# The scan's input products in pairs, with eight state buffers in place of six

## The chip, the cores and the metric

The kernel runs on one core of a Trainium2 chip. The metric is the device time of one launch in microseconds (us), the median of several runs. The engines are called by their names in the profile: PE (TensorE matmuls) and PEld (its weight loads), DVE (VectorE), ACT (ScalarE), POOL (GpSimd) and SP (SyncE, which issues all transfers). Each runs its own queue in order; they meet through semaphores.

## The reference

The reference is a network of two layers on x of 32 sequences x 256 tokens x 128 features, all in fp32. Each layer has the form

```python
h = layernorm(x) * (1 + ca) + sa;  x = x + ga * mixer(h)
h = layernorm(x) * (1 + cb) + sb;  x = x + gb * ffn(h)
```

with shifts, scales and gates per sequence. Layer 0: attention with 16 query heads, 4 key heads and a relative position bias, then a mixture of 16 experts with 4 picked per token. Layer 1: a selective scan over 256 channels x 16 states, then three chained matrices and a tanh. The scan is what the change touches:

```python
dA  = exp(dt[..., None] * A)
dBx = dt[..., None] * B_ssm[:, :, None, :] * x_conv[..., None]
# h[t] = dA[t] * h[t-1] + dBx[t]
y = einsum('btdn,btn->btd', h, C_ssm)
```

## The kernel before

The 32 sequences are worked in 16 pairs of 512 tokens (TOK). Every phase of a pair (attention `a_`, experts `m_`, scan `s_`, last block `f_`) is cut into small functions, one for each piece and engine. A written timetable puts each piece at a step: a pair starts every 128 steps (STEPS), and `AT` holds a due step relative to the pair's start for each function. Each engine walks over all steps from -101 to 2455 and emits what is due, in a fixed order within a step (`step_sync`, `step_gpsimd`, ...). A step is thus a place in a queue, not a time. Four pairs are in flight at a time: while pair p is scanned, pair p+1 goes through its experts and the pairs behind through attention. The last three pairs have tables of their own (`LAST_AT`, `LATE_SCAN`, `LATE_LAG`), since nothing new starts behind them.

The scan of a pair has 256 x 16 = 4096 rows of 512 tokens, which makes 32 batches of 128 rows. A row of the partition axis is a channel and a state: 16 channels x 8 states. One fetch (`s_fetch_sync`, L1145) brings dt and dt*x of 16 channels, each repeated on 8 partitions (512 KB), into a ring slot; the ring has four. A fetch serves two batches, one for each half s of the states: of eight batches the first four use fetches n to n+3 with s = 0, the next four the same fetches with s = 1. Batch m is due at step 388 + 27m/8 of its pair (at smaller numbers in the last two pairs). It consists of

- the fetch, due at lag -14 (-12 in the last three pairs). It waits until POOL's product (`s_dbx`) and ACT's decay (`s_da`) of the last batch of the slot's former contents are done.
- the decay on ACT (`s_decay_scalar`, L1186), lag -1: exp of dt times A into a PSUM bank. It waits for the scan of the batch before (of the one before that in the last two pairs, which have two banks).
- the input product on POOL (`s_input_gpsimd`, L1197), lag -3: (dt*x) times B into a state buffer `hb[at % HB]`. It waits for the fetch, for the row of B in `bc`, and for the sum that frees the buffer.
- the scan on DVE (`s_scan_vector`, L1203), lag +1, in place in the state buffer.
- the product with C, in place: on POOL (`s_read_gpsimd`, L1210), lag +4, or in the late pairs on DVE (`s_read_vector`, L1218).
- for every fourth batch, the sum of four batches over the states on PE (`s_sum_tensor`, L1233), lag +6. It frees four state buffers.

Other pieces named later: on POOL the experts' weighing (`m_weigh_gpsimd`, L929) and four root chains per pair (`ln_root_gpsimd`, L436 to L453: 16 dependent operations on 128x4 elements), due at steps 155 (b), -82 (a), 330 (n) and 517 (f) of their pairs; on ACT th (L900) and the attention's exp (L605); on DVE L907 and L922 of the experts, the routing (L759 to L814), L663, and the scan's end L1240 and L1242; on PE L872, L916 and L934 (the experts' matmuls) and L588 (scores). L1313 adds the last block to its input, L1317 stores it.

Of the kernel before, what the change touches and what calls it, by code (L numbers as in the profile page):

```python
# [9 lines left out]
ALU = mybir.AluOpType  # L10
# [3 lines left out]
P = 128  # L14
B, T, D = 32, 256, 128
PAIRS = B // 2
TOK = 2 * T
# [28 lines left out]
BATCHES = 32  # L46
HB = 6
XSLOTS = 3
RING = 4
# [18 lines left out]
def build(nc, dram, out, q_rows, w_rows_d, dt_rows, bc_rows):  # L68
    ctx = ExitStack()
    with ctx:  # L70
# [82 lines left out]
        bc = sb("bc", [P, 2 * SG, TOK])  # L153
        work = sb("work", [P, HB * TOK + RING * 2 * TOK])

        def cut(lo, n):
            return work[:, lo:lo + n]

        hb = [cut(k * TOK, TOK) for k in range(HB)]
        ring = [cut((HB + 2 * k) * TOK, 2 * TOK).rearrange("p (r t) -> p r t", r=2) for k in range(RING)]  # L160

        conv_s, conv_t = step[:, 0, :], step[:, 2, :]
        dt_s = [step[:, 0, :], step[:, 2, :]]
# [78 lines left out]
        s_in = [sem(f"s_in{k}") for k in range(RING)]  # L242
        s_da, s_dbx, s_h, s_hc, s_y, s_g, s_yv = (sem("s_" + n) for n in ("da", "dbx", "h", "hc", "y", "g", "yv"))
# [13 lines left out]
        def tokens(ap):  # L257
# [15 lines left out]
            x_res_sync=107, a_store_sync=-34, m_store_sync=178, m_fetch_sync=-13, s_rows_sync=377,  # L273
            s_rows_in_sync=[378, 380, 384, 386], s_store_sync=[372, 374], s_fetch_sync=-14, f_store_sync=531,
            a_scores_tensor=0, m_gate_tensor=1, m_up_tensor=3, m_down_tensor=9, a_turn_tensor=5, a_values_tensor=40,
# [13 lines left out]
            s_silu_vector=[352, 359], s_zgate_vector=[392, 401], f_res_vector=514, f_stats_vector=518, f_end_vector=533,  # L289
            s_read_gpsimd=4, m_weigh_gpsimd=5, s_input_gpsimd=-3, a_root_gpsimd=-82, b_root_gpsimd=155, s_root_gpsimd=330,  # L290
            f_root_gpsimd=517, s_step_vector=[366, 370],
# [50 lines left out]
        LATE_LAG = dict(s_decay_scalar=0, s_scan_vector=1, s_read_gpsimd=4,  # L342
                        s_input_gpsimd=-3, s_sum_tensor=6, s_fetch_sync=-12)

# [811 lines left out]
        def landed(p, n):  # L1156
            return 16 * (FETCHES // RING * p + n // RING + 1)
# [31 lines left out]
        def s_input_gpsimd(pool, p, m):  # L1189
            n, j, s = batch(m)  # L1190
            at = BATCHES * p + m
            if m in (0, 4):
                pool.wait_ge(bc_in[s], 16 * (p + 1))
            pool.wait_ge(s_in[n % RING], landed(p, n))
            if at >= HB:
                pool.wait_ge(s_y, (at - HB) // 4 + 1)
            nc.gpsimd.tensor_tensor(hb[at % HB], ring[n % RING][:, 1, :], bc[:, s, :], ALU.mult).then_inc(s_dbx, 1)  # L1197

# [425 lines left out]
        def step_gpsimd(pool, st):  # L1624
            at = batch_due("s_read_gpsimd", st)
            if at is not None and not copies(*at):
                s_read_gpsimd(pool, *at)
            at = expert_due("m_weigh_gpsimd", st)
            if at is not None:
                m_weigh_gpsimd(pool, *at)  # L1630
            at = batch_due("s_input_gpsimd", st)
            if at is not None:
                s_input_gpsimd(pool, *at)
            p = due("a_root_gpsimd", st)
            if p:
                ln_root_gpsimd(pool, LN_A, p)
            p = due("b_root_gpsimd", st)
            if p is not None:
                ln_root_gpsimd(pool, LN_B, p)
            p = due("s_root_gpsimd", st)  # L1640
            if p is not None:
                ln_root_gpsimd(pool, LN_S, p)
            p = due("f_root_gpsimd", st)
            if p is not None:
                ln_root_gpsimd(pool, LN_F, p)
# [241 lines left out]
```

## Time and profile before

| | us |
|---|---|
| median of 3 runs | 2771.68 |
| lowest and highest run | 2770.18, 2782.97 |
| span of the profiled execution | 2781.6 |

The profiled execution's own time is not given apart from its span; of the three times the highest lies 1.4 us above the span. The page gives busy times of the engines over the span, the costliest groups of instructions, and the idle time before each with its releaser. Shares over the whole span hide that the kernel has a long steady part (about 240 to 2400 us, one pair each 157 us) and an end of some 280 us in which no new pair comes in.

### The profile page before, as it was taken

How to read it: one execution, taken by the hardware profiler on the slowest of the kernel's cores; microseconds unless marked ns; L12 is line 12 of the kernel's file. 1: busy time of each engine (PE TensorE's matmuls, PEld its weight loads, DVE VectorE, ACT ScalarE, POOL GpSimd, SP SyncE). 2: the span in 40 equal slices, each digit the busy share in tenths (PEclk: the TensorE clock that was granted, in tenths of full speed). 3: DMA queues.
4: the chain of work that ended last, by engine and by line, in shares of the span. 5: the costliest groups of instructions: out<-in, count | busy, mean ns of one | idle time of the engine just before them, and what ended most of it. 6: DMA issues, size and time to landing. Idle time of an engine off the chain costs nothing. (4 is left out here: it accounts for less than half of the span.)

```text
span 2781.6 us, 37104 instructions
## 1 busy us (share of the span) xinstructions
PE 2360.3 (85%) x9792; PEld 1217.4 (44%) x9792; DVE 1947.1 (70%) x3193; ACT 1630.6 (59%) x4157; POOL 1717.8 (62%) x2235
## 2 busy tenths in 40 slices
PE   5889998989888999989899898988989898987533
PEld 3555544444444444444444444444444444432110
DVE  2445558686877868686776768677686867768776
ACT  3655656666666666666666665666666566643432
POOL 1012258585866858585776757587685757766643
PEclk9999999999999999999999999999999999998755
DMA  7424365565546565555556465554645555344542
GB/s 135 48 46 78 58 141 99 122 125 126 118 84 134 115 132 114 111 121 118 115 109 134 95 121 119 119 117 85 143 106 120 115 125 105 85 116 114 126 122 68
DMA packets 497980, 304.96 MB, mean 110 GB/s; under 512 B 349817, under 2 KB 416297, under 8 KB 497321
## 3 DMA queue, kind: packets, MB, share of 16 engines
q1 hardware_dynamic: 497772, 302.59, 53.4%
q8 instruction: 82, 1.34, 0.2%
q14 instruction: 126, 1.03, 0.1%
HBM read 242.21 MB, written 26.74 MB: 97 GB/s over the span
## 5 line engine op out<-in xcount | busy, mean ns | idle before, releaser
L1197 POOL TENSOR_TENSOR work<-work,bc 128x512 f32<-128x512 f32 x512 | 648.1, 1274 | 100.1 <-PE bank L1233 92.1
L1203 DVE TENSOR_TENSOR_SCAN work<-bank,work 128x512 f32<-128x512 f32 x512 | 621.3, 1213 | 96.4 <-POOL work L1197 74.7
L929 POOL TENSOR_TENSOR zh<-zh,w_bc 128x512 f32<-128x512 f32 x256 | 326.7, 1276 | 582.9 <-DVE zh L922 582.8
L1186 ACT ACTIVATE bank<-work,neg_a 128x510 f32<-128x510 f32 x512 | 351.5, 687 | 457.1 <-DVE work L1203 445.5
L1210 POOL TENSOR_TENSOR work<-work,bc 128x512 f32<-128x512 f32 x436 | 564.9, 1301 | 80.6 <-DVE work L1203 80.5
L588 PE MATMUL bank<-ke,q_all 96*128 96x256 f32 x2048 | 558.3, 396 | 12.1 <-DMA q_all<-q_rows 12.1
L605 ACT ACTIVATE probs<-bank,nmax 128x256 f32<-128x256 f32 x1024 | 473.7, 470 | 131.3 <-DVE nmax L595 129.3
L595 DVE TENSOR_REDUCE nmax<-bank 128x2 f32<-128x512 f32 x512 | 348.6, 681 | 229.6 <-PE bank L588 218.5
L588 PEld LDWEIGHTS bank<-ke,q_all 96*128 96x128 f32 x2048 | 384.3, 198 | 215.9 <-issue 164.6
L916 PE MATMUL bank<-h_b,w_t 128*128 128x512 f32 x512 | 296.9, 663 | 119.5 <-DVE zh L907 110.2
L615 PEld LDWEIGHTS bank<-ident,probs 128*128 128x128 f32 x2048 | 256.0, 144 | 241.9 <-issue 173.7
L623 ACT ACTIVATE probs_t<-bank 128x512 f32<-128x512 f32 x512 | 304.0, 594 | 85.9 <-PE bank L645 69.7
L615 PE MATMUL bank<-ident,probs 128*128 128x128 f32 x2048 | 318.9, 279 | 37.5 <-ACT probs_t L623 37.3
L907 DVE SCALAR_TENSOR_TENSOR zh<-th,bank 128x512 f32<-128x512 f32 x256 | 174.5, 682 | 233.2 <-ACT th L900 231.7
L872 PE MATMUL bank<-h_b,w_t 128*128 128x512 f32 x512 | 291.1, 651 | 0.0
L934 PE MATMUL bank<-zh,w_t 128*128 128x512 f32 x512 | 265.3, 600 | 0.9 <-POOL zh L929 0.9
L922 DVE SCALAR_TENSOR_TENSOR zh<-bank,b_c,zh 128x512 f32<-128x512 f32 x256 | 190.1, 743 | 74.5 <-PE bank L916 70.7
L900 ACT ACTIVATE th<-bank 128x512 f32<-128x512 f32 x256 | 152.1, 594 | 128.3 <-PE bank L872 126.9
L1233 PE MATMUL bank<-work,sel_d 128*32 128x512 f32 x1024 | 160.3, 661 | 73.0 <-DVE work L1218 62.1
L605 ACT ACTIVATION_READ_ACCUMULATOR probs<-bank,nmax 128x1 f32 x1024 | 206.7, 202 | 0.0
L916 PEld LDWEIGHTS bank<-h_b,w_t 128*128 128x128 f32 x512 | 82.1, 194 | 228.5 <-DVE zh L907 193.9
L934 PEld LDWEIGHTS bank<-zh,w_t 128*128 128x128 f32 x512 | 95.6, 191 | 129.3 <-issue 120.6
(193 smaller groups left out, 2537.8 us busy)
## 6 DMA issues: line engine op xcount, KB each, us to landing
work<-dt_rows SPq DMA_DIRECT2D x256, 512.0 KB, 5.3
w_bc<-w_rows_d SPq DMA_DIRECT2D x256, 256.0 KB, 4.5
ke<-ke SPq DMA_DIRECT2D x128, 256.0 KB, 5.0
bc<-bc_rows SPq DMA_DIRECT2D x64, 256.0 KB, 7.3
x_in<-in_x SPq DMA_DIRECT2D x32, 256.0 KB, 5.1
q_all<-q_rows SPq DMA_DIRECT2D x512, 8.0 KB
dt_rows<-step SPq DMA_DIRECT2D x16, 512.0 KB, 3.6
dt_rows<-step SPq DMA_DIRECT2D x32, 256.0 KB, 2.2
```

Of the source, the lines that this page charges most:

```text
L588: last = nc.tensor.matmul(bank[n % 2][:, k * T:(k + 1) * T], q_all[0:QROWS, i0 + k, :], ke_q[:, i0 + k, :], start=True, stop=True)
L595: nc.vector.tensor_reduce(nmax[:, 2 * c:2 * c + 2], bank[n % 2][:, :].rearrange("p (k t) -> p k t", k=2), AX_X, ALU.max, negate=True).then ...
L605: last = nc.scalar.activation(probs[:, n % 2, k, :], bank[n % 2][:, k * T:(k + 1) * T], ACT.Exp, bias=nmax[:, i:i + 1], accum_out=rsum[:, ...
L615: last = nc.tensor.transpose(tile(bank[2], 2 * kh + k), probs[:, n % 2, k, kh * P:(kh + 1) * P], ident[:, :])
L623: nc.scalar.activation(by_head, bank[2][:, :].rearrange("p (x c r) -> p x r c", x=4, r=H // G), ACT.Copy).then_inc(a_tc, 1)
L916: nc.tensor.matmul(up_bank(n)[:, :], w3_t[:, e, :], h_b[:, p % 2, :], start=True, stop=True).then_inc(m_u, 1)
L929: nc.gpsimd.tensor_tensor(zh[:, n % 3, :], zh[:, n % 3, :], w_bc[:, n % WB, :], ALU.mult).then_inc(m_p, 1)
L934: nc.tensor.matmul(bank[5][:, :], w2_t[:, e, :], zh[:, n % 3, :], start=False, stop=(e == NE - 1)).then_inc(m_w2, 1)
L1186: nc.scalar.activation(segments(decay_bank(p, m)[:, :])[:, :, 1:], segments(ring[n % RING][:, 0, :])[:, :, 1:], ACT.Exp, scale=neg_a[:, SG ...
L1197: nc.gpsimd.tensor_tensor(hb[at % HB], ring[n % RING][:, 1, :], bc[:, s, :], ALU.mult).then_inc(s_dbx, 1)
L1203: nc.vector.tensor_tensor_scan(hb[at % HB], decay_bank(p, m)[:, :], hb[at % HB], 0.0, ALU.mult, ALU.add).then_inc(s_h, 1)
L1210: nc.gpsimd.tensor_tensor(hb[at % HB], hb[at % HB], bc[:, SG + batch(m)[2], :], ALU.mult).then_inc(s_hc, 1)
```

## The change

The input products of batches m and m+1 (m even) become one POOL operation of 128x1024 elements. It reads the dt*x parts of two neighbouring ring slots, and the same row of B twice (by a broadcast), and writes two neighbouring state buffers; it adds 2 to `s_dbx` at its end. It waits for both fetches. It is emitted where the odd batch's product is due, at lag -7 instead of -3. The state buffers are eight instead of six (two more rows of 512 elements), and the fetches are due at lag -15 instead of -14, and -15 instead of -12 in the last three pairs. The scratch for transfers' descriptors is made smaller.

```diff
--- before.py
+++ after.py
@@ -44,7 +44,7 @@
 DC = 16
 SG = 2
 BATCHES = 32
-HB = 6
+HB = 8
 XSLOTS = 3
 RING = 4
 FETCHES = DI // DC
@@ -159,6 +159,13 @@
         hb = [cut(k * TOK, TOK) for k in range(HB)]
         ring = [cut((HB + 2 * k) * TOK, 2 * TOK).rearrange("p (r t) -> p r t", r=2) for k in range(RING)]
 
+        def hb_two(k):
+            return work[:, k * TOK:(k + 2) * TOK].rearrange("p (r t) -> p r t", r=2)
+
+        def ring_two(k):
+            lo = (HB + 2 * k) * TOK
+            return work[:, lo:lo + 4 * TOK].rearrange("p (k r t) -> p k r t", k=2, r=2)[:, :, 1, :]
+
         conv_s, conv_t = step[:, 0, :], step[:, 2, :]
         dt_s = [step[:, 0, :], step[:, 2, :]]
         dt_x = [step[:, 1, :], step[:, 0, :]]
@@ -271,7 +278,7 @@
             a_out_tensor=[79, 144], a_out_scalar=[79, 145], s_end_vector=[447, 499],
             a_spread_sync=[[-28, -28, -12, 4], [20, 36, 52, 68]], a_scatter_sync=[[-22, 4], [37, 69]], x_a_sync=-99,
             x_res_sync=107, a_store_sync=-34, m_store_sync=178, m_fetch_sync=-13, s_rows_sync=377,
-            s_rows_in_sync=[378, 380, 384, 386], s_store_sync=[372, 374], s_fetch_sync=-14, f_store_sync=531,
+            s_rows_in_sync=[378, 380, 384, 386], s_store_sync=[372, 374], s_fetch_sync=-15, f_store_sync=531,
             a_scores_tensor=0, m_gate_tensor=1, m_up_tensor=3, m_down_tensor=9, a_turn_tensor=5, a_values_tensor=40,
             a_inverse_tensor=41, s_sum_tensor=6, a_turned_tensor=-48, a_keys_tensor=-42, a_values_in_tensor=-37,
             a_query_tensor=-34, f_end_tensor=531, a_back_tensor=148, b_turned_tensor=157, m_logits_tensor=164,
@@ -287,7 +294,7 @@
             m_route_vector=[166, 166, 167, 167, 168, 168, 169, 169, 170, 170, 171, 171, 172, 172, 173, 173, 174, 174, 175, 175, 176],
             m_end_vector=327, s_stats_vector=329, s_conv_vector=[[349, 349, 350, 350], [357, 357, 358, 358]],
             s_silu_vector=[352, 359], s_zgate_vector=[392, 401], f_res_vector=514, f_stats_vector=518, f_end_vector=533,
-            s_read_gpsimd=4, m_weigh_gpsimd=5, s_input_gpsimd=-3, a_root_gpsimd=-82, b_root_gpsimd=155, s_root_gpsimd=330,
+            s_read_gpsimd=4, m_weigh_gpsimd=5, s_input_gpsimd=-7, a_root_gpsimd=-82, b_root_gpsimd=155, s_root_gpsimd=330,
             f_root_gpsimd=517, s_step_vector=[366, 370],
         )
 
@@ -340,7 +347,7 @@
                         m_up_vector=3, m_silu_vector=2, m_weigh_gpsimd=4, m_fetch_sync=-5)
         LATE_SCAN = {1: (364, 24), 2: (375, 27), 3: (388, 27)}
         LATE_LAG = dict(s_decay_scalar=0, s_scan_vector=1, s_read_gpsimd=4,
-                        s_input_gpsimd=-3, s_sum_tensor=6, s_fetch_sync=-12)
+                        s_input_gpsimd=-7, s_sum_tensor=6, s_fetch_sync=-15)
 
         def place(name, p, *k):
 
@@ -1192,9 +1199,11 @@
             if m in (0, 4):
                 pool.wait_ge(bc_in[s], 16 * (p + 1))
             pool.wait_ge(s_in[n % RING], landed(p, n))
-            if at >= HB:
-                pool.wait_ge(s_y, (at - HB) // 4 + 1)
-            nc.gpsimd.tensor_tensor(hb[at % HB], ring[n % RING][:, 1, :], bc[:, s, :], ALU.mult).then_inc(s_dbx, 1)
+            pool.wait_ge(s_in[(n + 1) % RING], landed(p, n + 1))
+            if at + 1 >= HB:
+                pool.wait_ge(s_y, (at + 1 - HB) // 4 + 1)
+            nc.gpsimd.tensor_tensor(hb_two(at % HB), ring_two(n % RING),
+                                    bc[:, s, :].unsqueeze(1).broadcast_to([P, 2, TOK]), ALU.mult).then_inc(s_dbx, 2)
 
         def s_scan_vector(dve, p, m):
             at = BATCHES * p + m
@@ -1629,8 +1638,8 @@
             if at is not None:
                 m_weigh_gpsimd(pool, *at)
             at = batch_due("s_input_gpsimd", st)
-            if at is not None:
-                s_input_gpsimd(pool, *at)
+            if at is not None and at[1] % 2:
+                s_input_gpsimd(pool, at[0], at[1] - 1)
             p = due("a_root_gpsimd", st)
             if p:
                 ln_root_gpsimd(pool, LN_A, p)
@@ -1870,7 +1879,7 @@
         "ffn_a2": f["L1_ffn_aux_weight2"], "ffn_b": f["L1_ffn_bias"][:, None], "ident": np.eye(P, dtype=one),
         "mask_d": mask_d, "sel_r": sel_r, "tie": tie, "sel_d": sel_d,
     }
-    nc = bacc.Bacc("TRN2", target_bir_lowering=False, num_devices=1)
+    nc = bacc.Bacc("TRN2", target_bir_lowering=False, num_devices=1, dynamic_dma_scratch_size=8192)
     dram, given = {}, {}
     for name, shape in IN_SHAPES:
         v = np.ascontiguousarray(arrays[name].reshape(shape))
```

## Rows read from the trace of the kernel before

**Rows 1.** The page: span and busy times
```profile
span 2781.6 us, 37104 instructions
...
PE 2360.3 (85%) x9792; PEld 1217.4 (44%) x9792; DVE 1947.1 (70%) x3193; ACT 1630.6 (59%) x4157; POOL 1717.8 (62%) x2235
```

**Rows 2.** Windows: stretch, busy PE, PEld, DVE, ACT, POOL, clock, DMA share
```profile
1300.00:1450.00 150.00, 137.59 (x590) 71.33 (x589) 110.39 (x186) 96.58 (x251) 109.55 (x141) 0.98 0.60 122
2600.00:2700.00 100.00, 35.71 (x112) 9.95 (x116) 83.56 (x112) 39.24 (x64) 50.59 (x74) 0.60 0.49 124
```

**Rows 3.** Waits from 240 to 2400 us: engine, line, cause: total us, times, longest
```profile
PE bank L916 <- DVE zh L907: 109.2, 85, 4.6
...
DVE work L1203 <- POOL work L1197: 56.3, 81, 2.5
...
POOL work L1197 <- PE bank L1233: 35.8, 49, 4.4
```

**Rows 4.** Timeline of one pair period: start, length, instruction, [idle before it]
```profile
1339.63 2.51 POOL L1197 TENSOR_TENSOR work<-work,bc 128x512 f32<-128x512 f32 x2
...
1358.40 1.22 DVE L1203 TENSOR_TENSOR_SCAN work<-bank,work 128x512 f32<-128x512 f32 x1 [1.44 <-POOL work L1197]
...
1363.12 1.26 POOL L1197 TENSOR_TENSOR work<-work,bc 128x512 f32<-128x512 f32 x1 [1.07 <-PE bank L1233]
...
1374.84 2.08 PE L916 MATMUL bank<-h_b,w_t 128*128 128x512 f32 x2 [2.23 <-DVE zh L907]
...
1418.68 1.23 DVE L1203 TENSOR_TENSOR_SCAN work<-bank,work 128x512 f32<-128x512 f32 x1 [1.22 <-POOL work L1197]
...
1420.53 1.12 PE L916 MATMUL bank<-h_b,w_t 128*128 128x512 f32 x2 [0.58 <-DVE zh L907]
```

**Rows 5.** Waits from 2400 us to the end
```profile
DVE work L1203 <- POOL work L1197: 18.4, 9, 4.0
```

**Rows 6.** Groups of POOL by line and form: busy us, mean ns, idle before
```profile
L1197 POOL TENSOR_TENSOR work<-work,bc 128x512 f32<-128x512 f32 x512 | 648.1, 1274 | 100.1 <-PE bank L1233 92.1 <-DMA work<-dt_rows 6.6 <-DMA bc<-bc_rows 0.8
...
L442 POOL TENSOR_TENSOR nw_b<-sd_b,rstd_b 128x4 f32<-128x4 f32 x48 | 9.6, 200 | 3.8
```

**Rows 7.** Timeline around one DVE operation with two SBUF operands
```profile
1368.04 1.27 POOL L1197 TENSOR_TENSOR work<-work,bc 128x512 f32<-128x512 f32 x1
1368.09 1.31 DVE L768 TENSOR_TENSOR ties<-gmax 128x64 f32<-128x64 f32 x1
```

**Rows 8.** Single source lines of DVE: count, ns min/median/max
```profile
L768 DVE TENSOR_TENSOR ties<-gmax x16: 217/1305/1307, 158.4 to 2500.0; 128x64 f32<-128x64 f32 x16
...
L1242 DVE SCALAR_TENSOR_TENSOR z_gate<-x_slots,d_par,z_gate x32: 751/752/4814, 447.0 to 2756.6; 128x512 f32<-128x512 f32 x32
```

**Rows 9.** Fetches (L1153): landing of the one issued at 2676.8, then the page
```profile
DMA to landing us min/median/max: 10.4/10.4/10.4
...
work<-dt_rows SPq DMA_DIRECT2D x256, 512.0 KB, 5.3
```

**Rows 10.** Timeline of the last two sequence pairs
```profile
2626.99 1.22 DVE L1203 TENSOR_TENSOR_SCAN work<-bank,work 128x512 f32<-128x512 f32 x1 [2.13 <-POOL work L1197]
...
2681.07 1.22 DVE L1203 TENSOR_TENSOR_SCAN work<-bank,work 128x512 f32<-128x512 f32 x1 [3.93 <-POOL work L1197]
...
2683.05 1.27 POOL L1197 TENSOR_TENSOR work<-work,bc 128x512 f32<-128x512 f32 x1 [2.01 <-DMA work<-dt_rows]
...
2684.78 1.21 DVE L1203 TENSOR_TENSOR_SCAN work<-bank,work 128x512 f32<-128x512 f32 x1
...
2703.69 1.22 DVE L1203 TENSOR_TENSOR_SCAN work<-bank,work 128x512 f32<-128x512 f32 x1 [3.99 <-POOL work L1197]
...
2711.53 0.69 DVE L1313 TENSOR_TENSOR x_b<-x_b,bank 128x512 f32<-128x512 f32 x1 [2.19 <-PE bank L482]
...
2744.39 1.22 DVE L1203 TENSOR_TENSOR_SCAN work<-bank,work 128x512 f32<-128x512 f32 x1
...
2746.24 1.22 DVE L1203 TENSOR_TENSOR_SCAN work<-bank,work 128x512 f32<-128x512 f32 x1
```

## The prediction

> **What bounds the kernel now.** I read the page first. PE is busy 2360.3 of 2781.6 us, the others 59 to 70% [rows 1]. The windows cut this in two. In the steady part (pairs 2 to 13) PE is busy 137.6 of 150 us at clock 0.98; from about 2500 us it falls to 35.7 of 100 while DVE holds 83.6 [rows 2]. So PE's work sets the pace for 13 pair periods, and each of its 12 idle us per period is lost time; at the end DVE's own chain of scans sets it. The waits, third, say what PE idles for: in the steady part its largest is L916 <- DVE L907, 109.2 us. DVE in turn idles 56.3 us before the scan L1203 for POOL's L1197, and POOL idles 35.8 us before L1197 for PE's sums L1233, the releaser of a state buffer [rows 3]. That is the chain the change touches: sum, buffer, input product, scan, then whatever DVE holds behind the scan.
>
> The timeline shows how much of DVE's 56.3 us reaches PE. In one period POOL waits 1.07 us for a buffer at 1363.12; scan 8 is 1.44 us late at 1358.40 and the next long wait of PE is 2.23 us at 1374.84; scan 23 is 1.22 us late at 1418.68, and L907, queued right behind it, costs PE 0.58 at 1420.53 [rows 4]. From 2400 us on, DVE idles 18.4 us for L1197 [rows 5].
>
> **The pair operation.** L1197 takes 1274 ns for 512 elements, the 4-element product of the same kind 200 [rows 6]: 1074/508 = 2.11 ns per element over a start. So 1024 elements should take 0.200 + 1020 x 0.00211 = 2.36 us. Back to back two old ones take 2.51 [rows 4]. I take 2.36, 0.15 less: 256 x 0.15 = 38 us of POOL, or 2.4 per pair. Its bounds: 2 x 1.27 = 2.55 if nothing is saved, and 2.9 if the two-level address pattern costs as much again as a start or two; below 2.1 is excluded, as the elements are as many. POOL is not the bound, so this alone is worth 0 to 1 us per pair; I count 0.
>
> **Its place and the buffers.** The distance from scan 8 (step 416) to scan 23 (step 466) is 60.3 us [rows 4], 1.21 us per step. With six buffers the product for batch 4k+6 needed the sum issued only 1.1 steps before; with eight, the pair (4k+8, 4k+9) needs one 7.2 steps before. So the 35.8 us of POOL's waits go. The even product ran 3 steps ahead of its batch; the pair now stands 3.6 to 4 ahead of the even and 7 ahead of the odd batch. For the even scan this is about neutral where POOL has a queue: some 0.6 step (0.7 us) earlier, 1.08 us longer. For the odd scan it is 3.6 steps (4.3 us) earlier, and its wait goes. Some pairs also change side with a four-element root chain (4.4 us of small POOL operations): (8, 9) at step 411 now precedes the root of the second norm, of the same step, and (22, 23) at 458 the third one. This frees scan 8 of its 1.44 us. What pays: the root chain, which the ACT norm and then PE wait for, has up to 2.36 us of POOL work before it. Pair (6, 7) and (8, 9) can use POOL's present idle time (the buffer waits and waits for DVE), so I charge 0.3 us, bounds 0 and 2.36. Reads (L1210) queued behind a pair are up to 1.1 us later; sum L1233 is two steps, 2.4 us, behind its read, which hides it; uncovered it would be 1.1 us of PE.
>
> **Steady sum.** Of the late scans of the period I give PE back: 1.1 of 2.23 us at 1374.84, 0.58 at 1420.53, and about 0.8 at three smaller places: 2.5 us, less 0.3 for the root chain, less 0.6 for longer blocking of DVE (below): 1.6 us. Times 13 periods: -20.8 us. Bounds per period: +3 (blocking) and -4.3 (all of 56.3/13).
>
> **The fetches.** A fetch is placed one step earlier (three in the last three pairs), but its second wait, for the decay that frees its slot, falls due at the same step as before. Fetch (n+1) for pair (8, 9) is now due at +15 steps, where decay 5 is due too; with 0.7 us decay and 5.3 us median landing [rows 9] it is there at about +20, and the pair is due at +23: 3.6 us of slack where the old even product had 6. So nothing in the steady part. On SP the wait starts a step earlier and holds what is queued behind: row loads of the experts (due 18 steps before use) and the small query loads (also well ahead); the store of the output now stands behind fetch 5 in place of ahead of it, which brings that fetch forward. At a pair's start fetch 0 now precedes the second half's store of dt rows, and waits for the first half's store while that one is not ready anyway. All 0. POOL issues no DMA, so the smaller descriptor scratch costs nothing; it and the two buffers are memory only.
>
> **The end.** DVE's chain of scans is closed here, 1.85 us per batch with its L1218 [rows 10], so a late pair is paid in full. Gains: the 2.13 us wait at 2626.99 goes (the pair now precedes a root chain), and half of the 8.35 us left of the 18.4 after the three waits I name: -6.3. The 3.99 at 2703.69 does not count: the chain through the last pair but one's end (root chain, L1313 waited for 2.19 us at 2711.53) ends later than these scans would. Losses: the last pair's scan 0 starts at 2681.07 after fetch 0 alone; the pair operation also needs fetch 1, which released POOL at 2683.05 [rows 10]. Late fetches queue for DMA (10.4 us from issue to landing, [rows 9]). With fetches 0 and 1 ahead of the third and fourth row loads in SP's order I put that landing at 2680.6: + 2.4 = 2683.0, 1.9 us later than 2681.07, and scan 1 moves alike; bounds 0 and +4.3 (fetch 1 not earlier). The pair before has the same with fetch 3: +1.5. At a ring refill, decay m-3 ends 7.25 us before scan m (five batches of 1.85, less scan, gap and decay), + 5.4 to land + 2.36: 0.5 us late, four uncovered times: +2. Fetch 5 before the root chain: +0.7. Together +6.1 - 6.3 = -0.2, bounds -12 and +13.
>
> **Total.** -20.8 - 0.2 = -21 us. Against the profiled span of 2781.6 this is 2760.6. Of the three times the slowest, 2782.97, lies 1.4 above that span and stands for such an execution; the median is 2771.68, 11.3 lower. I apply the difference to the median: 2751 us.
>
> **A rule that speaks against it.** A DVE operation with two SBUF operands is held while POOL works: L768 starts at 1368.09, 0.05 us after a POOL product, and ends at 1369.40, just after that one's end at 1369.31 [rows 7]; its median is 1305 ns where 217 is possible, and L1242 goes to 4814 ns from 751 [rows 8]. By the rows a blocked operation waits for the POOL operation's end, sometimes for several in a row; a pair would make the longest single wait 2.36 us, while there are half as many. Mean wait: chance of meeting the same, remainder twice as long (0.6 to 1.2 us), of which I charged 0.6 us per period above.
> The Trainium skill, in "SBUF — State Buffer", section "Who interferes with whom", says the port pair shared by VectorE and GpSimd is an exclusive lock held for the whole instruction, so the later one blocks fully. The trace agrees in L768. If the rule holds for every such operation and the pair's whole length, the sum would be rival A's.
>
> **Rivals.** A, slower: the port. In each period about five of DVE's two-operand operations are stretched now; if two meet a pair for its whole length and one more starves like L1242 (4.06 us over its 751 ns), DVE loses some 4 to 5 us per period and PE 3 (in the period shown PE's 2.23 us follow such stretches): +39 - 27 (the 2.1 of gains without the charge, 13 times) = +12 with +6 at the end: 2790. For it: the 4814 ns. Against: its median is 752. It decides from 2.1 us of PE per period on. B, no change: DVE's gained time stops at the next wait (for ACT's L900 or PE's scores), as PE is at 92% and has many small ones; 0.5 us per period, -6, and +6 at the end: 2772. C, full gain: ACT's decays, which wait for scans, come forward too and all 56.3 us return, with -4 at the end: 2711. D, the change does not do what it says: the pair takes 2.9 us, so POOL gets busier by 90 us and even scans are later: 2778.
>
> **Chances.** Forecast 0.42 (own range 2735 to 2767), B 0.22, A 0.20, C 0.11, D 0.05. The range 2720 to 2795 leaves out half of C and the far end of A. A change under 0.5% (13.9 us) could not be told from none: bounds 2757.8 and 2785.5. Faster: 0.30 of the forecast, C and a little of B: 0.43. Slower: most of A and ends of B and D: 0.21. Same: 0.36.
>
> **What would show it.** L1197 x256 at 2.36 us; DVE's steady wait for it from 56.3 to under 25, POOL's for L1233 to near 0; PE's wait L916 <- L907 from 109.2 to about 90; the 512 scans unchanged; the last pair's scan 0 at 1.9 us further behind its fetch. A is shown by medians of L768, L773 and L1242 well up; B by DVE's waits moved to L907 or L595 with PE idle as before. The forecast is wrong if L1197 takes over 2.6 us, or if POOL waits at its head for a fetch in the steady part.

## The result, and the profile after: 2.75% slower

The changed kernel takes 2847.4 us (2847.2 to 2848.2 in 4 runs), the kernel before 2771.5 (2770.2 to 2783.0 in 4); the ratio is 1.0275, with a 95% interval of 1.0252 to 1.0298. The prediction of 2751 us was wrong in sign and its range, up to 2795, did not hold the time. Medians here leave out two runs of experiments whose granted clock was lower than in the other runs of the same kernel, one of e1 (3485.7 us) and one of e10 (2805.1).

The page's head and two windows (columns: busy us and instructions of PE, PEld, DVE, ACT, POOL, then the granted clock, the DMA share and GB/s), against [rows 1, 2]:

```profile
span 2845.5 us, 36850 instructions
PE 2386.8 (84%) x9792; PEld 1226.7 (43%) x9792; DVE 1949.4 (69%) x3193; ACT 1630.4 (57%) x4157; POOL 1679.3 (59%) x1979
...
1300.00:1450.00 150.00, 132.27 (x552) 67.98 (x551) 108.50 (x182) 89.72 (x231) 99.36 (x121) 0.97 0.56 112
2600.00:2700.00 100.00, 63.82 (x182) 21.86 (x183) 79.55 (x109) 41.70 (x71) 65.38 (x66) 0.83 0.45 119
```

POOL is busy 38.5 us less than before, ACT as long, DVE 2.3 us longer. PE is busy 26.5 us longer: its matmuls are as many and take longer where its clock is lower. The span is 63.9 us longer, so the other 37.4 us are idle time of PE, and there the waits tell more. Those of the steady part, 240 to 2400 us (sum in us, times, longest), against [rows 3]:

```profile
PE bank L923 <- DVE zh L914: 115.2, 75, 4.2
DVE work L1212 <- POOL work L1205: 57.0, 49, 4.3
POOL work L1205 <- DMA work<-dt_rows: 40.5, 18, 3.4
DVE work L1212 <- ACT bank L1193: 36.5, 38, 3.4
```

(L1205 is the pair product, L1212 the scan, L1193 the decay, L914 and L923 are L907 and L916 of before.) POOL's wait for the sums, 35.8 us before, is gone from the list. A new one stands in its place: the pair product waits for a fetch, 40.5 us. DVE still waits 57.0 us for POOL, now seldomer and longer (49 times, up to 4.3 us, in place of 81, up to 2.5).

A pair's period, read as the distance between the starts of L1322 (L1313 before) for the second half of one pair and of the next, says where the time went. Two of the changed kernel:

```profile
1051.86 0.68 DVE L1322 TENSOR_TENSOR x_b<-x_b,bank 128x512 f32<-128x512 f32 x1
1215.99 0.68 DVE L1322 TENSOR_TENSOR x_b<-x_b,bank 128x512 f32<-128x512 f32 x1
1379.59 0.68 DVE L1322 TENSOR_TENSOR x_b<-x_b,bank 128x512 f32<-128x512 f32 x1
```

The profiled execution of before has two kinds of periods: six of its first eleven take 157.2 to 157.4 us and five 162.9 to 163.6, with a sum of 1760. In the changed kernel all eleven take 162.4 to 164.1, with a sum of 1800. The last four add up to 479.9 instead of 462.5, and the first pair is finished 6 us later: 40 + 17 + 6 is the 64 us between the spans. (The medians differ by more, 76 us, as the profiled execution of before was near the slowest of its four.)

One such period at its critical place, in the order of time on each engine (start, duration; in brackets the idle time before and who ended it):

```profile
1252.90 2.36 POOL L1205 TENSOR_TENSOR work<-work,bc 128x1024 f32<-128x1024 f32 x1
...
1258.90 2.36 POOL L1205 TENSOR_TENSOR work<-work,bc 128x1024 f32<-128x1024 f32 x1
...
1268.35 2.34 POOL L1205 TENSOR_TENSOR work<-work,bc 128x1024 f32<-128x1024 f32 x1 [3.41 <-DMA work<-dt_rows]
```
```profile
1270.73 1.22 DVE L1212 TENSOR_TENSOR_SCAN work<-bank,work 128x512 f32<-128x512 f32 x1 [4.29 <-POOL work L1205]
1271.87 0.66 DVE L602 TENSOR_REDUCE nmax<-bank 128x2 f32<-128x512 f32 x1
1272.45 0.68 DVE L914 SCALAR_TENSOR_TENSOR zh<-th,bank 128x512 f32<-128x512 f32 x1
```
```profile
1273.18 1.13 PE L923 MATMUL bank<-h_b,w_t 128*128 128x512 f32 x2 [4.24 <-DVE zh L914]
```

The pair of batches 18 and 19 waits 3.41 us for its second fetch, scan 18 another 2.34 for both halves of the product, L914 stands behind the scan, and PE idles 4.24 us. Then PE's clock falls from 1.00 to a mean of 0.66 over the next 5 us, as the windows there show (columns as above; 1.0 is the level of 2.4 GHz, 0.5 that of 1.2 GHz):

```profile
1268.00:1273.00 5.00, 0.95 (x6) 0.42 (x4) 2.27 (x3) 1.24 (x3) 4.65 (x3) 1.00 0.68 88
1273.00:1278.00 5.00, 4.82 (x16) 3.49 (x17) 4.96 (x6) 2.01 (x8) 5.00 (x4) 0.66 0.01 2
1278.00:1283.00 5.00, 5.00 (x26) 1.46 (x24) 4.24 (x13) 3.72 (x10) 4.67 (x7) 1.00 0.63 111
```

That adds 5 x 0.34 = 1.7 us of matmul time to the idle 4.24. The whole period beside a short one of before (the first row is before, the second the changed kernel):

```profile
1032.97:1190.21 157.24, 142.90 (x610) 74.13 (x610) 115.98 (x193) 101.05 (x260) 113.40 (x144) 0.99 0.58 118
```
```profile
1215.99:1379.59 163.60, 146.44 (x610) 75.84 (x610) 117.70 (x193) 101.10 (x260) 110.51 (x129) 0.97 0.58 114
```

Of the 6.4 us between them PE is busy 3.5 us longer, with the same 610 matmuls at a lower clock, and idle 2.8 us longer. So more than half of the loss is time at the lower level. The changed kernel has two such stretches in this period, about 1245 and 1273 us (the first follows 2.57 us of idle time), the short period of before has one shorter one.

Why that fetch is late, SP's queue shows (issue time; DMA_DIRECT2D is a transfer):

```profile
1250.75 5.09 SPq L1160 DMA_DIRECT2D work<-dt_rows  x2
1256.01 0.47 SPq L843 DMA_DIRECT2D w_rows_d<-ke  x1
1260.15 0.35 SPq L851 DMA_DIRECT2D w_bc<-w_rows_d  x1
1260.59 0.63 SPq L579 DMA_DIRECT2D ke<-ke  x1
1261.32 0.55 SPq L1160 DMA_DIRECT2D work<-dt_rows  x1
```

The second of the two L1160 at the top is the fetch for batch 18. Its slot is free when the product of pair (14, 15) has ended at 1255.26, and being one operation this tells it only there. Behind it stands the small store of the experts' weights, L843 (32 KB), which lands 4.1 us after its issue; the load behind that, L851, waits 3.6 us for it; and only behind the load comes the fetch for batch 19, at 1261.32. The decay that its slot also waits for had ended at 1257.30, 4.0 us earlier. The fetch lands 6.8 us after its issue. In the kernel before the store was issued 0.43 us ahead of a fetch and landed in 1.6 us, and products told their end singly:

```profile
1386.52 0.33 SPq L836 DMA_DIRECT2D w_rows_d<-ke  x1
1386.95 0.51 SPq L1153 DMA_DIRECT2D work<-dt_rows  x1
```

SP's wait for the store, over the steady part, is 42.9 us in the changed kernel (the first row) and 8.5 in the kernel before (the second):

```profile
SPq L851 <- DMA w_rows_d<-ke: 42.9, 13, 3.9
```
```profile
SPq L844 <- DMA w_rows_d<-ke: 8.5, 14, 1.2
```

At the end, the last pair's scan 0 waits 6.95 us for its pair product, 3.93 before [rows 10], and POOL's idle time before it, 19.24 us, ended with a fetch:

```profile
2738.73 2.34 POOL L1205 TENSOR_TENSOR work<-work,bc 128x1024 f32<-128x1024 f32 x1 [19.24 <-DMA work<-dt_rows]
```
```profile
2741.11 1.22 DVE L1212 TENSOR_TENSOR_SCAN work<-bank,work 128x512 f32<-128x512 f32 x1 [6.95 <-POOL work L1205]
```

Over the last four periods together the scans wait no longer for products than before (17.1 us in place of 21.3), but 18.5 us for ACT's decays, where it was 7.7 before. How the 17.4 us divide among these places was not traced further.

### The profile page after: what moved, and what is told of

Same layout as the page of the kernel before. It is cut to its first block, busy times and chain, and to the rows that moved or that the text cites. A ratio compares the mean times of both kernels' runs of the same rounds, so it can differ in the third digit from the quotient of the medians.

```text
span 2845.5 us, 36850 instructions
## 1 busy us (share of the span) xinstructions
PE 2386.8 (84%) x9792; PEld 1226.7 (43%) x9792; DVE 1949.4 (69%) x3193; ACT 1630.4 (57%) x4157; POOL 1679.3 (59%) x1979
## 4 chain that ended last, share of the span: by engine, by line
PE 41%; issue 15%; POOL 14%; DVE 13%; ACT 9%; DMA 7%; SPq 1%; POOLq 0%; ACTq 0%; DVEq 0%
PE bank L595 9%; PE bank L923 5%; DMA work<-dt_rows 5%; PE bank L879 5%; POOL work L1205 4%; POOL work L1219 4%; PE bank L622 3%; PE bank L652 2%; DVE work L1212 2%; PE bank L1041 2%; DVE zh L914 2%; PE bank L697 2%; PE bank L1242 2%; ACT th L907 2%; ACT probs L612 2%
## 5 line engine op out<-in xcount | busy, mean ns | idle before, releaser
L1212 DVE TENSOR_TENSOR_SCAN work<-bank,work 128x512 f32<-128x512 f32 x512 | 621.3, 1213 | 128.2 <-POOL work L1205 74.0
L1205 POOL TENSOR_TENSOR work<-work,bc 128x1024 f32<-128x1024 f32 x256 | 603.9, 2362 | 116.3 <-DMA work<-dt_rows 113.5
L1193 ACT ACTIVATE bank<-work,neg_a 128x510 f32<-128x510 f32 x512 | 351.5, 687 | 507.0 <-DVE work L1212 504.2
L1219 POOL TENSOR_TENSOR work<-work,bc 128x512 f32<-128x512 f32 x436 | 561.6, 1299 | 110.0 <-DVE work L1212 110.0
L923 PE MATMUL bank<-h_b,w_t 128*128 128x512 f32 x512 | 301.2, 672 | 128.3 <-DVE zh L914 119.7
L914 DVE SCALAR_TENSOR_TENSOR zh<-th,bank 128x512 f32<-128x512 f32 x256 | 175.0, 684 | 250.4 <-ACT th L907 248.7
L879 PE MATMUL bank<-h_b,w_t 128*128 128x512 f32 x512 | 293.0, 655 | 0.0
L1242 PE MATMUL bank<-work,sel_d 128*32 128x512 f32 x1024 | 164.2, 677 | 83.7 <-DVE work L1227 64.0
L907 ACT ACTIVATE th<-bank 128x512 f32<-128x512 f32 x256 | 152.1, 594 | 137.8 <-PE bank L879 136.2
L923 PEld LDWEIGHTS bank<-h_b,w_t 128*128 128x128 f32 x512 | 83.9, 199 | 236.7 <-DVE zh L914 199.7
```

What stands on the lines that cost most here:

```text
L879: nc.tensor.matmul(gate_bank(n)[:, :], w1_t[:, e, :], h_b[:, p % 2, :], start=False, stop=True).then_inc(m_g, 1)
L923: nc.tensor.matmul(up_bank(n)[:, :], w3_t[:, e, :], h_b[:, p % 2, :], start=True, stop=True).then_inc(m_u, 1)
L1193: nc.scalar.activation(segments(decay_bank(p, m)[:, :])[:, :, 1:], segments(ring[n % RING][:, 0, :])[:, :, 1:], ACT.Exp, scale=neg_a[:, SG ...
L1205: nc.gpsimd.tensor_tensor(hb_two(at % HB), ring_two(n % RING), bc[:, s, :].unsqueeze(1).broadcast_to([P, 2, TOK]), ALU.mult).then_inc(s_db ...
L1212: nc.vector.tensor_tensor_scan(hb[at % HB], decay_bank(p, m)[:, :], hb[at % HB], 0.0, ALU.mult, ALU.add).then_inc(s_h, 1)
L1219: nc.gpsimd.tensor_tensor(hb[at % HB], hb[at % HB], bc[:, SG + batch(m)[2], :], ALU.mult).then_inc(s_hc, 1)
```

## The experiments

All were compared with the kernel before on the same chip, whose median moved from 2768 to 2775 us between the groups of runs; so a difference of a few us between two kernels of different groups says little, and the ratios go before the medians. "Steady" is the mean of the first eleven pair periods of the profiled execution, "last four" their sum at the end.

| kernel | us | ratio (95%) | steady | last four |
|---|---|---|---|---|
| before | 2768 to 2775 | 1 | 160.0 | 462.5 |
| changed | 2847.4 | 1.0275 (1.0252 to 1.0298) | 163.6 | 479.9 |
| e1 fetches at -14/-12 | 2943.0 | 1.0603 (1.0570 to 1.0636) | 171.3 | 489.3 |
| e2 two singles in the pair's place | 2782.0 | 1.0025 (1.0000 to 1.0050) | 159.6 | 468.9 |
| e3 before, eight buffers | 2784.5 | 1.0055 (1.0023 to 1.0087) | 159.7 | 463.7 |
| e4 before, fetches at -15 | 2773.9 | 0.9998 (0.9969 to 1.0028) | 159.3 | 461.9 |
| e5 singles, both wait for both fetches | 2791.2 | 1.0077 (1.0049 to 1.0106) | 159.5 | 472.2 |
| e6 singles, one signal at the end | 2802.8 | 1.0106 (1.0068 to 1.0143) | 160.4 | 470.1 |
| e7 singles, e5 and e6 together | 2847.6 | 1.0259 (1.0214 to 1.0305) | 163.8 | 481.1 |
| e8 changed, six ring slots | 2808.3 | 1.0126 (1.0089 to 1.0163) | 160.5 | 477.3 |
| e12 e8, singles in the last three pairs | 2797.0 | 1.0097 (1.0064 to 1.0130) | 160.6 | 464.0 |
| e13 changed, L843 a step earlier | 2823.4 | 1.0193 (1.0149 to 1.0237) | 161.2 | 477.9 |
| e14 e12, pair at -6 | 2839.9 | 1.0239 (1.0204 to 1.0274) | 164.3 | 468.8 |
| e9 before, scan's end through PSUM | 2794.9 | 1.0086 (1.0056 to 1.0117) | 161.1 | 462.5 |
| e10 before, six ring slots | 2774.7 | 1.0021 (0.9990 to 1.0051) | 160.1 | 462.2 |
| e11 e9 and e10 together, fetches at -15 | 2795.3 | 1.0091 (1.0058 to 1.0125) | 161.0 | 462.6 |
| e15 before, scan's end two steps later | 2827.8 | 1.0199 (1.0164 to 1.0233) | 163.4 | 463.5 |

### Which part of the change: e1 to e4

The edits below are cut to what matters, and some are written in short words in place of the code. e1 puts the fetches back to their old lags and keeps the rest:

```diff
-s_fetch_sync=-15   (late pairs: s_fetch_sync=-15)
+s_fetch_sync=-14   (late pairs: s_fetch_sync=-12)
```

> The changed kernel with the fetches due at lag -14 (-12 in the last three pairs) again; pair products at lag -7 and eight buffers stay. Theory Q (queue order): at -15 the fetch for batch 18 goes out ahead of the small store of the expert weights, whose landing then takes 3.9 us in place of about 1.6; the expert's row load and the fetch for batch 19 queue behind it, that fetch goes out 2.8 us later, and the pair product (18, 19) waits 3.41 us. With -14 the stall of PE there (4.24 us) should fall under 1.5 us, the period go from 163.8 back to about 157.5 and the time to 2760 to 2785. Theory M (merging: the pair needs the later of two fetches, wherever they are queued): most of the stall stays, 2820 to 2845. Theory P (the 2.36 us operation holds DVE at the shared port): 2830 to 2847, unchanged.

It is 96 us slower than the changed kernel, outside the ranges of all three theories. So the new fetch lag is no fault but a mitigation: the pair needs its second fetch earlier, and one step less of lead costs 7.7 us in each period. In e1's waits POOL stands 98.4 us for fetches (longest 7.3), and since it then reaches the root chains late, PE stands up to 8.0 us for y_a:

```profile
PE bank L923 <- DVE zh L914: 100.1, 73, 3.2
PE bank L472 <- ACT y_a L465: 88.0, 13, 8.0
```

e2 keeps lags, buffers and places, and writes the pair as two operations, each with its own wait and its own signal:

```diff
-            nc.gpsimd.tensor_tensor(hb_two(...), ring_two(...), ...).then_inc(s_dbx, 2)
+            for k in range(2):
+                pool.wait_ge(s_in[(n + k) % RING], landed(p, n + k))
+                ...
+                nc.gpsimd.tensor_tensor(hb[(at + k) % HB], ring[(n + k) % RING][:, 1, :], bc[:, s, :], ALU.mult).then_inc(s_dbx, 1)
```

> The changed kernel with two products of 512 elements in place of one of 1024, emitted at the same place, each waiting for its own fetch and buffer; lags -15 and -7 and eight buffers stay. Theory Q: the fetch for batch 19 is as late as before, but only product 19 waits for it; the work behind scan 18 goes on, while POOL and scan 19 are still held: 2785 to 2830. Theory M: the stall was made by the merging, 2755 to 2780. Theory P: no long operations, 2755 to 2780 too, with DVE's two-operand operations short.

It falls from 2847 to 2782: merging the two operations costs 65 us, everything else in the change 7 (0 to 14 by the interval). Its scans show where the gain that I forecast would have gone:

```profile
DVE work L1211 <- ACT bank L1193: 46.8, 38, 3.7
DVE work L1211 <- POOL work L1205: 1.5, 1, 1.5
```

The wait for POOL, 56.3 us before [rows 3], is down to 1.5, and the one for ACT's decays is up from 14.8 to 46.8. The steady period is 159.6 us, 160.0 before: next to nothing was gained. (One of its eleven periods took 167.0 us; in it the scan's end, L1250 here, took 7.15 us. On this see the last experiments.)

e3 gives the kernel before eight buffers alone; e4 gives it the earlier fetches alone:

> The kernel before with eight state buffers alone (and the smaller scratch). All theories: POOL's 92.1 us of waits for PE's sums go. If those waits reach the end, 2750 to 2765; if DVE's time comes back at the next wait, 2768 to 2775. Periods that still last 163 us would show another cause than the buffers.

> The kernel before with the fetch lags of the change alone (-15, also in the last three pairs). Theory Q: the same order of store and fetches, but product 19 has four steps more before it is due, so that only part of the 2.8 us shows: 2775 to 2810, more of its periods at 163 us. Theories M and P: no change, 2765 to 2775.

Neither gains anything: e3 is 0.2 to 0.9% slower, which no theory had, and e4 is not told from the kernel before, as theories M and P had it. In e3 POOL's waits for the sums are gone and DVE still waits 55.3 us for L1197, 84 times: the products were late by POOL's queue, not by the buffers.

### Which property of merging: e5 to e7

A merged operation differs from two in three ways: its first half waits for the second fetch too, it tells the end of both halves only at the end, and it holds POOL 2.36 us in one piece. e5 has the first alone, e6 the second, e7 both, all without the long operation:

```diff
 # e5                                      # e6                               # e7
+wait both fetches                        +wait fetch n                      +wait both fetches
+product(m).then_inc(s_dbx, 1)            +product(m)                        +product(m)
+product(m + 1).then_inc(s_dbx, 1)        +wait fetch n + 1                  +product(m + 1).then_inc(s_dbx, 2)
                                          +product(m + 1).then_inc(s_dbx, 2)
```

> As the changed kernel, but the pair is again two operations of 512 elements back to back; both stand behind the waits for both fetches, each adds 1 to s_dbx at its own end. This has only the first property of the pair, the wait for the second fetch ahead of the first product. Theory W (that wait is the fault: at 1268.35 the pair waited 3.41 us for its second fetch, the scan behind it 4.29 and PE 4.24): 2835 to 2850 us, pair periods of 163 to 164, POOL's waits for transfers 90 us or more. Theory G (the one signal at the pair's end is the fault, since the next fetch of the slot and the even scan wait for it): about 2782, as the two singles without either property gave. Theory L (the long operation itself): about 2782 too.

> As the changed kernel, but two operations of 512 elements, the first waiting for its own fetch only, the second for its own; s_dbx is raised by 2 at the end of the second, not at all by the first. This has only the second property, the late signal (and with it the even scan also waits for the second fetch, but POOL's other work does not stand behind a wait before the first product). Theory W in its narrow form (POOL held before the first product): about 2782 to 2790. Theory G (late signal): 2835 to 2850, with periods of 163 to 164. Theory L: about 2782.

> As the changed kernel, but the one operation of 1024 elements is replaced by two of 512 between the same waits and the same single signal at the end; POOL pays 2.5 us in place of 2.36 per pair (19 us more in all). Only the long operation is taken away. Theories W and G: 2840 to 2855, the same as the changed kernel or up to 10 more. Theory L (length of one operation, its hold on DVE's operands): about 2785.

e7 gives the changed kernel's time, 2847.6, without a long operation in it (ratio 1.0259, with an interval of 1.0214 to 1.0305, beside 1.0275). So the length does not cause the loss, and rival A is out as its cause. It is not without effect: DVE is busy 1949.4 us in the changed kernel and 1923.9 in e7, but the time does not follow (e7's POOL is busy 35.5 us longer, so strictly the two together are worth nothing). Above e2's 2782, in medians, the wait alone costs 9 us, the signal alone 21, both together 66; by the ratios 14, 22 and 65. Neither theory W nor G alone was right, and their costs do not add. PE's waits for L914 in e2, e5, e6 and e7, in this order (sum, times, longest), go with it:

```profile
PE bank L923 <- DVE zh L914: 76.8, 70, 6.3
```
```profile
PE bank L923 <- DVE zh L914: 77.8, 74, 2.2
```
```profile
PE bank L923 <- DVE zh L914: 87.8, 71, 2.6
```
```profile
PE bank L923 <- DVE zh L914: 99.9, 69, 4.7
```

(The longest of e2, 6.3 us, is out of line with its small sum.) The late signal issues the fetch for batch 18 later, and with it everything behind it on SP: from the start of the products (14, 15) to the issue of the fetch for batch 19 pass 7.1 us in e2 and 6.9 in e5, but 8.4 in e6, 8.3 in e7 and 8.4 in the changed kernel. The wait for both fetches then passes that on to POOL, to scan 18 and to PE. The store behind the fetch is late in all of them (SP waits 36.7 us for it in e2); only with the merged waits and signal does it reach PE. In e7 the PE operation behind the stall takes 2.08 us where the one before takes 1.13, at half the clock again:

```profile
1259.77 1.13 PE L923 MATMUL bank<-h_b,w_t 128*128 128x512 f32 x2
1270.00 2.08 PE L923 MATMUL bank<-h_b,w_t 128*128 128x512 f32 x2 [3.12 <-DVE zh L914]
```

From 600 to 2200 us the mean granted clock is 0.99 in e2, e5 and e6 and 0.97 in e7 and the changed kernel.

### Whether it is the fetch: e8, e12, e13, e14

e8 gives the changed kernel six ring slots, so that a fetch waits for products two to six batches older; e12 also returns to single products at the old lags in the last three pairs; e14 puts e12's pair one step later.

```diff
-RING = 4
+RING = 6
-            return 16 * (FETCHES // RING * p + n // RING + 1)
+            return 16 * ((FETCHES * p + n) // RING + 1)
```

> The changed kernel with six ring slots in place of four (the fetches stay at lag -15; descriptor scratch 4096). A fetch then waits for products and decays two to six batches older, so it is issued when it is due and not when the last product of the slot's former contents has ended. Theories W and G (the second fetch is late because its slot is free late, and the pair needs it early): POOL's waits for transfers fall from 113 us to under 30, periods back to 157 to 158 and the time to 2750 to 2785. Theory L (long operation): stays at 2835 or more.

e8 gives back 39 of the 65 us. In its steady part POOL waits 3.9 us for fetches instead of 40.5 and every period is 160.0 to 161.3; the last four stay long (477.3). The forecast of 2750 to 2785 was too good. Of the 26 us that it still stands above e2, the last four periods make 8, the eleven steady ones 10 and the time up to the first pair's end 4, of which the cause was not separated further.

> The changed kernel with six ring slots (2808 us), and in the last three pairs single products at their old place again (lags -3 and -12). The last four pair periods were 477.3 us there, 462.5 in the kernel before. If pairing and the lag -7 cost at the end what they cost there because DVE's chain waits for the whole pair at each fetch: the last four periods return to 463 to 467, the time to 2793 to 2799, while the steady periods stay at 160 to 161. If the end's loss has another cause (eight buffers, the changed order of the steady part): 2803 to 2810.

As foretold: the last four return from 477.3 to 464.0, and 2797 is inside the interval named. So 13.3 of the end's 17.4 us come from the pairs and their earlier place there, and not from the buffers or the order of the steady part; six slots alone had given 2.6.

e13 moves one small transfer of the changed kernel, to tell whether a single fetch decides:

```diff
-m_store_sync=178
+m_store_sync=177
```

> The changed kernel, with the store of the experts' weights (L843) one step earlier, so that SP issues it ahead of the fetch for batch 18 and not behind it; nothing else. In the changed kernel the load behind it (L851) waits 3.6 us for that store and the fetch for batch 19 stands behind the load. If the loss turns on that one fetch: it is issued some 2 to 3 us earlier, the pair's wait of 3.41 us and PE's of 4.24 go, the second stretch at half clock goes from most periods, periods fall from 164 to 160 to 161 and the time to 2800 to 2815. If the loss is spread over all refills of the ring: 2840 or more.

It gives 24 us back, 2823.4 (8 us more than the range named), with steady periods of 161.2. L851's wait for the store falls from 42.9 us to 8.4, as in the kernel before, and the store lands in 1.6 us again, so it was the fetch in front that delayed it, and the two fetches stand 2.3 us apart:

```profile
1245.66 0.32 SPq L843 DMA_DIRECT2D w_rows_d<-ke  x1
1246.08 0.52 SPq L1160 DMA_DIRECT2D work<-dt_rows  x1
1247.24 0.34 SPq L851 DMA_DIRECT2D w_bc<-w_rows_d  x1
1247.67 0.63 SPq L579 DMA_DIRECT2D ke<-ke  x1
1248.41 0.55 SPq L1160 DMA_DIRECT2D work<-dt_rows  x1
```
```profile
1256.63 2.35 POOL L1205 TENSOR_TENSOR work<-work,bc 128x1024 f32<-128x1024 f32 x1 [1.54 <-DMA work<-dt_rows]
```
```profile
1261.48 1.13 PE L923 MATMUL bank<-h_b,w_t 128*128 128x512 f32 x2 [2.38 <-DVE zh L914]
```

The pair waits 1.54 us instead of 3.41, PE 2.38 instead of 4.24, and the operation behind runs at full clock. So the place of one store of 32 KB, once a period, makes 2.4 of the 4.0 us that a period of the changed kernel lies above one of e2; six slots make 3.1 of them. (The two were not run together.)

> The kernel with six ring slots, pairs in the steady part and single products in the last three pairs (2797 us), with the pair one step later in POOL's queue (lag -6 in place of -7). If what is left of its cost (periods of 160.5, two singles at the same place 158.9, singles at the old place 157.2) comes of the pair standing ahead of reads, weighings and root chains that are due earlier: periods of 159 to 160, 2780 to 2790. If it comes of the even batch, which gets its product later than from a single: periods of 161 or more, 2800 to 2815.

A miss on the side of its second theory, and by more than it said: 2839.9, with periods of 164.3. DVE's wait for the pair product goes from 13.9 us in e12 to 125.7 (83 times): at -6 the even batch gets its product late each time. The pair is thus held from both sides: at -6 its even half is late even with six slots, and at -7 with four slots its odd half's fetch is (40.5 us of waiting in the steady part, 5.6 in e12). Single products at -3 leave DVE 56.3 us of waiting there [rows 3] and give periods within 0.4 us of e2's.

### The two periods of the kernel before: e9, e10, e11, e15

In the long periods of before, L1242 (two operands in SBUF) starts beside POOL's back-to-back operations and ends when POOL stops for want of work. PE stands for L907 behind it and then runs at half clock; the window behind it gives 0.50:

```profile
761.70 4.81 DVE L1242 SCALAR_TENSOR_TENSOR z_gate<-x_slots,d_par,z_gate 128x512 f32<-128x512 f32 x1
```
```profile
768.87 2.08 PE L916 MATMUL bank<-h_b,w_t 128*128 128x512 f32 x2 [4.64 <-DVE zh L907]
```
```profile
768.00:773.00 5.00, 4.13 (x9) 2.63 (x10) 4.74 (x7) 2.62 (x9) 3.40 (x3) 0.50 0.00 0
```

The two go together without exception in this execution: each of the five long periods has an L1242 of 4.81 us, and in the six short ones it takes at most 1.15. It is so in e3 and e4 too.

e9 sends the first operation's result through PSUM, so that L1242 has one SBUF operand; e15 moves both two steps later.

> The kernel before, with the scan's end written so that its second operation has one operand in SBUF: L1240 writes its product into PSUM bank 7 in place of z_gate, and L1242 reads it there (PE's next sums wait for L1242 instead of L1240, 0.8 us later). Theory S (the kernel before has two kinds of pair periods, 157.2 and 163.4 us, because in the long ones L1242 is held 4.81 us by POOL's operations, PE stands 4.64 us for L907 queued behind, and runs at half clock after it): L1242's longest falls from 4814 to under 1000 ns, nearly all periods are 157 to 158, the time 2740 to 2760 and its runs agree better. The rival (L1242's hold is only where a shortage shows that has another cause): periods stay mixed, 2765 to 2780.

> The kernel before with the scan's end (L1240, L1242) two steps later in DVE's queue. If its long periods come from L1242 meeting a row of back-to-back POOL operations at that place (held 4.81 us): the share of 163 us periods changes, to none if POOL's queue has run dry there (2740 to 2755), or to all if it is always met (2790 or more), and L1242's longest tells which. If the two kinds have another cause: still mixed, 2765 to 2780.

e9 missed the 2740 to 2760 of theory S, and its rival's range as well. L1242 takes 746 to 749 ns everywhere there, and the 157 us periods are gone as well as the 163 us ones; they are 159.0 to 162.3. The hold was removed and the time was not won: PE now waits 27.3 us, 11 times, before L482 without a single releaser that the profile names. What that is was not followed up. In e15 L1242 takes up to 4.21 us and ten of eleven periods are long (163.5 to 163.9), the second of the two outcomes named. Together they show that the place where the scan's end meets POOL decides between short and long periods; that the hold alone is the cause of the long ones is not shown, and e9 speaks against it.

> The kernel before with six ring slots in place of four and nothing else (descriptor scratch 4096), to see what the ring alone is worth. If single products never wait for a slot in the steady part (POOL waited for transfers 6.6 us in all there), it is worth nothing in the steady part and some us at the end: 2755 to 2775. If the ring itself gave the 39 us that separate the pair with six slots from the pair with four, it would give them here too: 2735.

Six slots alone are worth nothing, as expected if single products hardly ever wait for a slot. e11, the two together with the fetches at -15, was a candidate for a faster kernel: 2735 to 2755 was expected if the slow periods went, 2765 to 2780 if not. It gave 2795.3, e9's time and outside both. None of the fifteen beats the kernel before.

## Why the prediction was wrong, by its steps

- **The pair operation** was right: 2362 ns for 1024 elements against the 2.36 us worked out from the two rows of POOL groups [rows 6], and POOL 38.5 us less busy.
- **Its place and the buffers**: the waits for sums went as forecast. That they were worth something was wrong (e3: nothing). By the timetable the odd product moves 4 steps forward (-3 to -7), not 3.6; this changes nothing in the sum.
- **The steady sum** of -20.8 us fell. I gave PE back late scans one by one [rows 4]. e2, which has all of the earlier products and none of the merging, turns 56.3 us of waiting for POOL into 46.8 for ACT and keeps its periods at 159.6. That is rival B's mechanism (the gain stops at the next wait), though the next wait is that for ACT's decays and not the ones B named; its 2772 stands beside e2's 2782.
- **The fetches** is the step that failed in the main part: "it is there at about +20, and the pair is due at +23: 3.6 us of slack where the old even product had 6. So nothing in the steady part." I worked it for pair (8, 9) only, where the slot is free by a decay, and took the median landing. The critical pair is (18, 19). I had left out that the merged product is also what frees the slot (its signal now comes at its end), that SP's queue between the pair's two fetches holds a store and a load that waits for it, and that a landing there takes 6.8 us, not 5.3. The quoted slack of 3.6 us was used up and 3.41 us of waiting stood above it. In the sum the step stood at nothing; merging measured 65 us (e7 and e2). The text named this as what would make it wrong; it had the condition and gave it no chance.
- **What a stall of PE costs**: I counted idle time at its length. Behind the 4.24 us of idle the clock fell and added 1.7 us (in e7, behind 3.12, 2.08 us for 1.13), and over a whole period the lower clock makes 3.5 of the 6.4 us. e5 and e6, with stalls up to 2.6, kept a mean clock of 0.99.
- **The end** was forecast at -0.2 with +13 as its bound, and measured +17.4. The direction of "losses" was right; the last pair's scan 0 waits 3.0 us more than before, not 1.9, and of the -6.3 of gains little came: the scans wait 4.2 us less for products over the last four periods and longer for decays. e12 puts 13.3 of the 17.4 on the pairs and their place.
- **Rivals**: A, the port, gave the nearest time (2790) for the wrong reason: L1251's longest is 2586 ns, 4814 before, DVE is busy 2.3 us longer in all, and e7 has the same time without a long operation. None of the four had a pair that waits for its own second input. That rival could be written from the diff alone: the first half of a merged operation waits for the second's input, and its user waits for the second's end.

The Trainium skill, in "SBUF — State Buffer", section "Who interferes with whom", has the shared ports as an exclusive lock, so that the later operation is blocked for the whole of the earlier one. L768 showed this [rows 7]; L1242 at 761.70 did not: it was held over four POOL operations that followed each other without a gap, 4.06 us over its own 751 ns.

## What to carry to other kernels

Merging two operations saves one start (here 0.15 us of 2.51) and ties their inputs and outputs: the first half starts with the later input and the first user waits for the last output. Before merging, take the later input's arrival for every instance, through its slot's release and through all that stands in front of it in the issuing queue, and not its median for one. And when an engine at 90% stalls, count the time after the stall too.

## What the runs showed of the hardware that was not expected

- PE idle for 4.24 us was followed by 5 us at a mean granted clock of 0.66, idle for 2.38 us (in e13) by an operation at full clock. In the kernel before, 2.23 us of idle were followed by a matmul pair of 2.08 us in place of 1.12 at 1374.84 [rows 4], so the length of the idle stretch alone does not decide.
- A store of 32 KB issued right behind a fetch of 512 KB landed in 4.1 us, and its follower waited 3.6 us for it. Ahead of the fetch it landed in 1.6 us (before, e13), and the follower's longest wait was 1.2 us. The medians of all 16 stores are 3.9 us in the changed kernel and 1.6 in the one before.
- A DVE operation of two SBUF operands was held by a row of POOL operations to 4.81 us (to 7.15 in e2) where it takes 0.75 alone, and periods of 157.2 and of about 163.4 us go with it in one and the same execution. The kernel before scattered from 2753 to 2790 us over 25 runs, the changed one from 2847.2 to 2848.2 over 4; that the mixture of periods makes this scatter is likely (six us a period) but was not traced run by run.
